# Attention and routed experts on one core: K in one product with its copies arranged by transfers, and routing per single batch within one step

## What is computed

```python
x = x + _L0_xattn_ref(_layernorm(x), ctx_1024, mask, Wq, Wk, Wv, Wo)   # 16 heads of 8, 64 keys a batch
x = x + _L0_ffn_ref(_layernorm(x), gate_w, wi_gate, wi_up, wo)         # 8 experts, F = 512, top 2
# routing: for each choice k: the token's rank among those that chose the same expert
onehot = (eid[:, None] == experts[None, :]).astype(jnp.int32)
pos_all = jnp.cumsum(onehot, axis=0) - 1
valid = pos < capacity                                                 # capacity 640 = 4096 / 8 * 1.25
disp = jnp.zeros((E, capacity, D)).at[eid, pos_c].add(jnp.where(valid[:, None], x_flat, 0.0))
expert_out = einsum(silu(disp @ wi_gate.T) * (disp @ wi_up.T), wo)
out = out + jnp.where(valid[:, None], ew[:, None] * expert_out[eid, pos_c], 0.0)
```

## Time and profile before

| | us |
|---|---|
| median of 3 runs | 385.34 (385.32 to 386.65) |
| the profiled execution | 385.02 |
| its span | 383.2 |

### The profile page before, as it was taken

One profiled execution on the slowest core, in us unless ns is written; L12 is line 12 of the kernel. 1 busy time (PEld: TensorE's weight loads), 2 busy tenths in 40 slices (PEclk: granted clock), 3 DMA queues, 4 the chain that ended last, 5 costly groups with the idle time before them and its releaser, 6 DMA issues.

```text
span 383.2 us, 8985 instructions
## 1 busy us (share of the span) xinstructions
PE 348.0 (91%) x3013; PEld 304.9 (80%) x3013; DVE 251.2 (66%) x933; ACT 193.4 (50%) x439; POOL 228.4 (60%) x195
## 2 busy tenths in 40 slices
PE   5899799999999996668999999999999999999970
PEld 2566577687778764558999999999999999999970
DVE  5898999999999996604455554645546455465440
ACT  3578677787888873303344444434434343344320
POOL 6373512667667777740464573864848638368673
PEclk9899999999999998598999999999999999999995
DMA  6899301222323222124137245463373544724232
GB/s 179 244 359 297 92 7 23 63 67 67 82 55 118 72 66 68 53 60 124 15 30 168 33 42 162 37 150 54 37 173 34 114 82 38 176 21 38 28 34 21
DMA packets 41159, 34.33 MB, mean 90 GB/s; under 512 B 8337, under 2 KB 37521, under 8 KB 40977
## 3 DMA queue, kind: packets, MB, share of 16 engines
q1 hardware_dynamic: 26592, 23.67, 21.0%
q0 software_dynamic: 13568, 9.58, 18.2%
q10 hardware_dynamic: 960, 0.60, 0.6%
HBM read 21.12 MB, written 17.73 MB: 101 GB/s over the span
## 4 chain that ended last, share of the span: by engine, by line
PE 68%; DVE 14%; POOL 6%; issue 4%; ACT 3%; DMA 3%; SPq 1%; POOLq 1%; DVEq 0%; ACTq 0%
PE bank L921 18%; PE bank L676 11%; PE bank L678 10%; PE bank L677 10%; PE bank L779 5%; POOL slots L441 4%; DVE mneg L1027 4%; PE bank L747 3%; PE bank L770 2%; PE bank L912 2%; DVE rall L1077 1%; PE bank L797 1%; DMA maskr<-in_mask 1%; PE bank L730 1%; PE bank L731 1%
## 5 line engine op out<-in xcount | busy, mean ns | idle before, releaser
L475 POOL DMA_INDIRECT out<-ys,idx x80 | 125.0, 1562 | 83.8 <-DVE ys L1308 52.1
L1335 DVE TENSOR_TENSOR h<-sg,bank 128x256 f32<-128x256 f32 x160 | 66.2, 419 | 86.8 <-ACT sg L661 78.7
L661 ACT ACTIVATE sg<-bank 128x256 f32<-128x256 f32 x160 | 61.5, 385 | 107.7 <-PE bank L678 107.2
L676 PE MATMUL bank<-ex_hi,w_hi 128*128 128x256 f32 x320 | 95.8, 299 | 1.0 <-DVE ex_lo L1289 0.3
L678 PE MATMUL bank<-ex_lo,w_hi 128*128 128x256 f32 x320 | 89.5, 280 | 0.0
L677 PE MATMUL bank<-ex_hi,w_lo 128*128 128x256 f32 x320 | 89.5, 280 | 0.0
L921 PE MATMUL bank<-w_raw,h 128*128 128x128 f32 x640 | 78.0, 275 | 0.8 <-DVE h L1335 0.8
L921 PEld LDWEIGHTS bank<-w_raw,h 128*128 128x128 f32 x640 | 74.9, 192 | 0.9 <-DVE h L1335 0.9
L441 POOL DMA_INDIRECT slots<-rall,slot x64 | 62.7, 980 | 18.4 <-issue 17.5
L676 PEld LDWEIGHTS bank<-ex_hi,w_hi 128*128 128x128 f32 x320 | 60.9, 190 | 4.1 <-issue 2.5
L677 PEld LDWEIGHTS bank<-ex_hi,w_lo 128*128 128x128 f32 x320 | 61.0, 190 | 0.0
(11 more groups left out here) (122 smaller groups left out, 536.7 us busy)
## 6 DMA issues: line engine op xcount, KB each, us to landing
slots<-in_empty SPq DMA_DIRECT2D x8, 660.0 KB, 10.7
xl<-slots SPq DMA_DIRECT2D x7, 660.0 KB, 7.3
w_raw<-in_wgu SPq DMA_DIRECT2D x8, 512.0 KB, 3.7
w_raw<-in_wdn SPq DMA_DIRECT2D x8, 256.0 KB, 4.3
out<-X SPq DMA_DIRECT2D x16, 128.0 KB
X<-in_x SPq DMA_DIRECT2D x3, 512.0 KB, 5.5
out<-ys,idx POOLq DMA_INDIRECT x80, 3.3
slots<-rall,slot POOLq DMA_INDIRECT x64
```

The source lines that it names most:

```text
L475: nc.gpsimd.indirect_dma_start(out=out[:, :], out_offset=bass.IndirectOffsetOnAxis(ap=IDX[v][:, j:j + 1], axis=0), in_=YS[c][:, t, :], in_ ...
L661: nc.scalar.activation(SG[m % 2][:], GATE_PS[m % 2][:, 0:2 * P], ACT.Silu).then_inc(sg_ready, 1)
L676: nc.tensor.matmul(ps, hi, m_hi, start=True, stop=False)
L1335: nc.vector.tensor_tensor(H[n % 2][:, f, :], SG[m % 2][:], UP_PS[m % 2][:, 0:2 * P], ALU.mult).then_inc(h_ready, 1)
```

## The change

K is projected with 128 columns, one product in three parts for a half (project_keys(0) in the start, (1) in step 1). Its high part is copied over the masked context in CTXM, its low part into CTX_LO, and nine transfers (three pieces by three parts) arrange both into KC, whose layout becomes row, group, batch, key. The host orders the weight's columns so that a partition of the product is column c of group g at 4c + g. place_keys issues one transfer per batch. SyncE issues the pieces for batches 0 to 7 before the loads of x, and waits for the last ones ahead of the first place_keys. All blocks are single batches; the chain of a block, with its ranks and ScalarE's exponential, stands in one step; the ranks go into M1 (bank 7), where turn2 waits until they are read. The parts of context and moments in the start change places.

```diff
-BLOCKS = [(0, 2), (2, 2), (4, 2), (6, 2)] + [(b, 1) for b in range(8, 16)]
+BLOCKS = [(b, 1) for b in range(B)]
 ROUTED = {first + n + 2: m for m, (first, n) in enumerate(BLOCKS)}
-RT = 4
-SENDS = {5: 4, 6: 3, 7: 5, 8: 3, 9: 5, 10: 4, 11: 5, 12: 5, 13: 5, 14: 5, 15: 4, 16: 4, 18: 12}
+RT = 2
+SENDS = {3: 3, **{b + 3: 4 for b in range(1, B - 1)}, B + 2: 5}
...
-PLACED = 16 * 4 * HG
+PLACED = 16 * 4 * HG * 2
...
-        KC = s1("kc", [P, B, GROUPS, LK])
+        KC = s1("kc", [P, GROUPS, B, LK])
...
-        K_PS = [MX[0], MX[1], DEN_PS, M1, M1, M1, M1, M1]
+        K_PS = M1
...
             for g in range(GROUPS):
-                sp.dma_start(KC[ONE_ROW:ONE_ROW + 1, :, g, :], EXT[:]).then_inc(ext_in, 16)
+                sp.dma_start(KC[ONE_ROW:ONE_ROW + 1, g, :, :], EXT[:]).then_inc(ext_in, 16)
+
+            def arrange_keys(piece):
+
+                b0, b1 = ((0, 2), (2, 8), (8, 16))[piece]
+                sp.wait_ge(k_used, b0 // 8 + 1)
+                for part in range(3):
+                    keys = CTXM[:, b0:b1, :] if part < 2 else CTX_LO[:, b0 * LK:b1 * LK].bitcast(F32)
+                    sp.dma_start(KC[32 * part:32 * part + 32, :, b0:b1, :], keys).then_inc(kc_in[piece], 16)
+
+            arrange_keys(0)
+            arrange_keys(1)
             for q in range(1, 4):
                 sp.dma_start(X[:, 8 * q:8 * q + 8, :], x_t[:, 8 * q:8 * q + 8, :]).then_inc(x_in[q + 1], 16)
...
                 sp.wait_ge(st_full, 4 * (2 * j - KBUF + 2))
                 for part in range(4):
                     for h in range(HG):
                         rows = slice(32 * part + DPH * h, 32 * part + DPH * h + DPH) if part < 3 else slice(ONE_ROW, ONE_ROW + 1)
-                        sp.dma_start(KS[rows, to, :, h * LK:(h + 1) * LK].bitcast(F32), KC[rows, b, :, :]).then_inc(done, 16)
+                        for b in (2 * j, 2 * j + 1):
+                            sp.dma_start(KS[rows, b % KBUF, :, h * LK:(h + 1) * LK].bitcast(F32), KC[rows, :, b, :]).then_inc(done, 16)
...
-            sp.wait_ge(k_used, 8)
+            arrange_keys(2)
+            for piece in range(1, 3):
+                sp.wait_ge(kc_in[piece], 48)
             sp.wait_ge(ext_in, 64)
             for j in range(3, B // 2):
                 place_keys(j)
...
-            pool.wait_ge(k_used, 4)
+            pool.wait_ge(kc_in[0], 48)
             pool.wait_ge(ext_in, 64)
             spread_keys(0)
...
+            def keys_hi(half):
+
+                act.wait_ge(k_full, half + 1)
+                nc.scalar.copy(CTXM[:, 8 * half:8 * half + 8, :].rearrange("p b k -> p (b k)").bitcast(F32R), K_PS[:]).then_inc(k_hi, 1)
...
             def rank(m, i):
                 pe.wait_ge(oh_ready, m + 1)
                 wait(pe, seen_ready, m)
-                wait(pe, rk_used, m)
-                if there(i - 1):
-                    pe.wait_ge(newton_step, 2 * i - 1)
+                pe.wait_ge(x1_ready, min(i - 1, B))
                 pe.wait_ge(tables, 1)
...
                 if there(i + 1):
                     select(i + 1, 1)
+                if i in ROUTED:
+                    rank(ROUTED[i], i)
                 if there(i - 1):
                     values(i - 1, 0).then_inc(pv_full, 1)
                 if there(i + 1):
                     row_scores(i + 1, 0)
-                if i in ROUTED:
-                    rank(ROUTED[i], i)
```

More of the change, by code:

```diff
@@ L223, in program @@
         k_full, k_hi, k_used = sem("k_full"), sem("k_hi"), sem("k_used")
+        kc_in = [sem(f"kc_in{v}") for v in range(3)]
         v_full, v_used = sem("v_full"), sem("v_used")
@@ L446, in step @@
                 if i + 2 < KBUF:
+                    wait(pool, kc_in[1], 48)
                     spread_keys(i + 2)
@@ L786, in sums @@
                 wait(pe, at_ready, b)
-                wait(pe, rk_used, sum(at <= b for at in ROUTED))
                 values(b, 1).then_inc(den_full, 1)
@@ L837, in _ @@
             keep_warm(WARM0[1])
-            for n in range(4):
-                project_keys(n)
+            project_keys(0)
+            pe.wait_ge(any_ready, 1)
+            project_values(0)
             pe.wait_ge(const_in, 16)
@@ L1198, in _ @@
             norm(1)
-            for n in range(1, 4):
-                keys_lo(n)
             queries_lo(0)
-            mask_context(1)
             moments(1)
-            context_lo(1)
             row_max(0, 0)
             def step(i):
-                now, last = ROUTED.get(i), ROUTED.get(i - 1)
+                m = ROUTED.get(i)
                 if there(i):
                     row_max(i, 1)
-                if last is not None:
-                    if last == 0:
-                        dve.wait_ge(tables, 3)
-                    own_ranks(last)
                 if i == 0:
@@ L1228, in step @@
                     add_input(i - 2)
-                if last is not None:
-                    limits(last)
-                if now is not None:
-                    best(now, 1)
+                if m is not None:
+                    which(m, 0)
                 if there(i - 2):
                     statistics2(i - 2)
-                if last is not None:
-                    places(last)
-                if now is not None:
-                    best(now, 0)
+                if m is not None:
+                    which(m, 1)
@@ L1239, in step @@
                 if there(i - 2):
                     moments2(i - 2)
-                if now is not None:
-                    which(now, 0)
+                if m is not None:
+                    one_hot(m)
                 if there(i - 2):
                     variance2(i - 2)
-                if last is not None:
-                    weight_sums(last)
-                    seen(last)
-                    past(last)
-                    weight1(last)
-                if now is not None:
-                    which(now, 1)
+                if m is not None:
+                    difference(m)
+                    added(m)
@@ L1252, in step @@
                 if there(i + 3):
                     norm(i + 3)
-                if last is not None:
-                    weight2(last)
-                    final(last)
-                if now is not None:
-                    one_hot(now)
+                if m is not None:
+                    limits(m)
                 if there(i - 1):
                     errors(i - 1)
+                if m is not None:
+                    if m == 0:
+                        dve.wait_ge(tables, 3)
+                    own_ranks(m)
@@ L1261, in step @@
                 if there(i - 2):
                     norm2(i - 2)
+                if m is not None:
+                    places(m)
                 if there(i - 1):
                     refine(i - 1)
-                if now is not None:
-                    added(now)
-                if i in (0, 1):
-                    keys_lo(2 * i + 5)
+                if m is not None:
+                    weight_sums(m)
+                    past(m)
+                if i == 0:
+                    context_lo(1)
```

102 lines of the change are left out of this document (43 added, 59 removed).

## The result

| | kernel before | changed kernel |
| --- | --- | --- |
| median of the runs, us | 385.33 (384.23 to 386.65) | 427.51 (426.41 to 427.81) |
| profiled execution, span, us | 383.2 | 424.6 |
| its mean granted clock of TensorE | 0.96 | 0.91 |

The changed kernel takes 1.109 times as long, with an interval of 1.107 to 1.112. The forecast was 419 us, from 400 to 430.

A forecast was written before the change was run, and what follows sets the result against it. TensorE and VectorE were taken as full in each steady step, SyncE's queue as 86% filled and the next bound. 385.0 + 36.2 (late keys) - 4 (end) + 1.5 (clock) = 418.7, plus 0.3 to the median: 419 us, range 400 to 430.

The forecast's parts named there:

- (a): SyncE's placed-key issues, 32 a pair instead of 16: cost is per instruction, 21.8 us a pair, SyncE becomes the bound.
- (b): Start of SyncE's first placing group: waits for the third arranged piece, queued behind the bulk; 50.5 us instead of 39.59.
- Rival A: Third piece passes the bulk or lands early, so SyncE's groups start near 40: 408 us, chance 0.12.
- (c): Sum for the keys: fifth group lands at 164.2 us against 128.03, so everything from step 13's end comes 36.2 later.
- (d): K's product in the start and steps 0 and 1: between a gain of 3 and a loss of 1.5, nothing in time.
- (e): Single-batch routing on VectorE, steps 3 to 11: 4 us more, hidden by late keys; about 3 without that cover.
- (f): Whole routing chain in one step, ranks waiting for the one-hot: 0 to 0.3 us a step, taken as 0.
- (g): End of the first part: last send 3.6 us earlier, warm-up and first rows meet; gain 4 us, from 2 to 5.
- (h): TensorE's granted clock after the waits for keys: 1.5 us added for the last group, from 0 to 3.
- B: Issues get cheaper with the transfer's shape, yet not enough, 0.50 to 0.60 us each: 396 us, chance 0.08.
- C: SyncE keeps up, with issues at 0.475 us or less: 382 us, between 379 and 386, chance 0.09.

The follow-up runs named there:

- e1: Kernel before with only the placed-key transfers issued per batch, 32 a pair instead of 16, from K's old layout: 418.23 us, ratio 1.085.
- e7: Changed kernel with the four weight transfers issued behind the first group of placing transfers, not ahead of the third arranging piece: 423.78 us, ratio 1.098.
- e3: Changed kernel with the third arranging piece's three transfers issued by ScalarE at the end of step 1, not by SyncE: 425.16 us, ratio 1.103.
- e6: Kernel before with the key part alone: K in one product, copies arranged by transfers, 16 issues a pair kept, old routing: 384.83 us, ratio 0.9986.
- e5: Kernel before with the routing part alone: single-batch blocks, chain in one step, new table of sends, keys as before: 382.90 us, ratio 0.9929.
- e8: Changed kernel with 40 products of unread result on TensorE ahead of its wait for batch 14's keys: 426.25 us.
- e10: Changed kernel with 26 products of unread result on TensorE ahead of its wait for batch 14's keys: 424.80 us, ratio 1.102.
- e2: Changed kernel with 16 issues a pair again, K for batches 6 to 15 arranged by batch in a second buffer: 382.83 us, ratio 0.9934.

## Why the prediction was right or wrong

**(a) The price of an issue: right in kind, 4% low.** I had 0.69 us from start to start for the transfers over 8 partitions and 0.655 for those over one, 21.8 a pair. A group has 22.3 to 23.0. The trace gives 0.718 for the former and 0.61 for the latter: 24 x 0.718 + 8 x 0.61 = 22.1. Half the bytes and half the runs took nothing off 0.728: e1 halves both in the old layout, and an issue over 8 partitions still lasts 0.685 us in its trace, and starts 0.728 after the last. The 10 ns came with the new layout of K. I had placed these issues midway between the 8-partition and the 1-partition transfer; the shape that hardly changed, 8 partitions, was the nearer row and should have kept its price. Over five groups and the last landing the dearer issues are 3.4 of the 5.3 us by which the keys are later than forecast; the other 1.9 are (b). e1 shows the term alone. The lower end of the forecast was also added up wrongly: issues of 0.655 are 21.0 us a pair, 4.2 less in all, thus 414.8 where it says 417; the range doesn't rest on it.

**(b) The first group at 52.37, forecast 50.5: the number nearly, by luck in part, the reason not.** The piece was issued at 34.3, not at 36, and landed 16.5 us after its last issue. The bulk was later than I had it: the mask transfers left 0.5 us later and not 1.6, but the last weight transfer at 30.05 and not at 28.4, and it landed at 50.6 and not at 47.4. That the piece comes behind the bulk is shown by e7; that it does so by its place in the queue was wrong, as e3 shows. The rule of ring order in the Trainium skill, DMA: Bandwidth & Descriptors, section "Queues, rings and completion order", which I had put beside it, decides nothing here: it is about one ring, and from another ring the piece was through only 1.4 us earlier. Within SyncE's queue the last landings keep that order, 50.6 for the weights and 52.3 for the piece. Rival A is out, and moving the piece to another queue would not have brought it about.

**(c) The sum.** 36.2 forecast, 41.5 measured, by the two terms above.

**(d) K in one product: nothing, right.** Beside late keys it is hidden, and without them e6 measures -0.4 us, with an interval that holds zero.

**(e) Single batches: nothing here, right, 1.5 and not 3 without the cover.** Only the stretch from step 3 to 4 shows it in the changed kernel (8.62 against 8.03), ahead of the first wait for keys. e5 shows why my 3 was too high: I had taken VectorE's free 0.15 us a step for all steps alike, but it is the bound only in the three stretches that hold moments.

**(f) The chain in one step: right.** TensorE waits for the one-hot twice, 1.4 us at most, in steps 17 and 18 where nothing else is left to do.

**(g) The end: 4.2 less, forecast 4.** The last send starts 29.8 us behind the scores (15, 0) where it was 32.8, 3.0 earlier of 3.6. The warm-up and the rows meet, and the 1.0 us of clock came as forecast. In e5 the same term is 3.3.

**(h) The clock behind the last wait: 4.15, forecast 1.5, bound 3.** This is the term that failed outright. I scaled it from a stretch of 3.3 us at 0.61 that followed a pause of 3.79. The stretch after a pause of 5.2 us is 6.8 us at 0.50, and it falls on a step in which TensorE has no slack, so the whole of it counts: at half the clock 6.8 us hold 3.4 us of a full clock's work, and the 4.7 us behind them, at 0.74, would lose 1.2 more, 4.6 in all by this estimate for the 4.15 measured. e8 and e10 show the term alone: the step is back to 7.34 and 7.26 us. The four waits before the last cost no such thing, because the next keys are late anyway.

Together, from the 418.7 us of the sum for one execution: 418.7 + 5.3 + 2.65 - 0.2 = 426.45, and the profiled execution has 426.41. The rivals B and C needed an issue under 0.6 us; none over 8 partitions was under 0.67.

## What to carry to other kernels

Here a transfer within SBUF cost its queue nearly the same whatever its size (0.57 us for 1 KB, 0.69 for 16 KB), so count issues, not bytes, and hold the count against the time between two uses; a queue that is filled to 86%, as this one was, can't take a loop that issues twice as often. When a layout makes a transfer fall apart into more transfers, pay for it once, while the data is arranged, as e2 does with 24 issues, and not in every round. Behind a pause of some us that lies ahead of full steps, add the time that the lower clock takes from steps without slack: here 4 us behind a pause of 5.

## What the runs showed of the hardware that I had not expected

- Starts of issues within SBUF over 8 partitions were 0.728 us apart, with 64 runs (the kernel before) as with 32 (e1), and 0.718 with 32 runs from the new layout; over one partition 0.61 with 4 runs and, for the last of a group's four, 0.67 with 8.
- A transfer of 768 KB within SBUF, issued at 35.4 to 37.4 us from ScalarE's queue, which had nothing else, wasn't through before 50.99, beside the slot fill and the weights issued up to 30.5 us in SyncE's: nothing of it moved before 40 us, and from 44 to 48 the two queues had equal numbers of packets. With the weights (1.5 MB) away it took 10.8 us instead of 16.5, in SyncE's queue.
- After 5.2 us without a matmul the granted clock was 0.50 for 6.8 us; after 26 products that filled the pause up to its last 0.2 us it was 1.00 throughout; after 20 products that ended 4.4 us ahead of the keys it fell to 0.50 in the one execution that was traced.
